# Readout of the memory as two rounded products, and a new order of the last stage's steps

## The reference, cut to what matters

```python
x = x + attention(_layernorm(x), ...)
x = x + xattn(_layernorm(x), ctx, mask)
x = x + ffn(_layernorm(x), ...)

def xattn(h, memory, mask):                      # h [8,512,512], memory [8,64,512]
    scores = einsum('bsd,bmd->bsm', h, memory) / sqrt(D)
    attn = softmax(where(mask, scores, -1e30))
    readout = einsum('bsm,bmd->bsd', attn, memory)
    return where(any(mask), readout, 0)

def ffn(x):
    qx, sx, sc = reorder_quantize(x)             # rounded to FP8, a scale for each row
    t = silu(qx @ w_gate) * (qx @ w_up)          # 1408 columns, each with its scale
    qt, st, sct = reorder_quantize(t)
    return qt @ w_down
```

## Time and profile before

| what | us |
|---|---|
| median of 3 runs | 2697.77 (2696.01 to 2700.08) |
| the profiled execution's own time | 2699.37 |
| its span | 2697.6 |
| mean granted TensorE clock | 0.991 of full |
| TensorE / VectorE / ScalarE / GpSimd busy | 2625.0 / 2123.9 / 1066.4 / 772.8 |

### The profile page before, as it was taken

One profiled execution on the slowest core, in us unless ns is written; L12 is line 12 of the kernel. 1 busy time (PEld: TensorE's weight loads), 2 busy tenths in 40 slices (PEclk: granted clock), 3 DMA queues, 4 the chain that ended last, 5 costly groups with the idle time before them and its releaser, 6 DMA issues.

```text
span 2697.6 us, 39827 instructions
## 1 busy us (share of the span) xinstructions
PE 2625.0 (97%) x14231; PEld 2173.0 (81%) x14231; DVE 2123.9 (79%) x3806; ACT 1066.4 (40%) x1786; POOL 772.8 (29%) x952
## 2 busy tenths in 40 slices
PE   6999899999999999999999999999999999999995
PEld 6888788888888888888888888888877666666662
DVE  7888977877787778778788867876657888888887
ACT  4433333433343343334344423433324445444553
POOL 3111211221131122112212211211123555555555
PEclk9999999999999999999999999999999999999998
DMA  6553322243233324343334422342265555555532
GB/s 230 180 212 141 128 104 104 102 163 121 102 136 131 122 100 137 105 147 119 126 111 147 157 94 94 118 180 94 94 227 173 148 157 161 151 147 160 162 99 54
DMA packets 182499, 366.67 MB, mean 136 GB/s; under 512 B 79264, under 2 KB 82208, under 8 KB 173600
## 3 DMA queue, kind: packets, MB, share of 16 engines
q1 hardware_dynamic: 116480, 339.74, 36.4%
q10 hardware_dynamic: 63488, 15.74, 3.2%
q0 software_dynamic: 2336, 8.65, 1.0%
HBM read 251.75 MB, written 96.61 MB: 129 GB/s over the span
## 4 chain that ended last, share of the span: by engine, by line
PE 95%; DVE 2%; issue 2%; POOL 0%; DMA 0%; ACT 0%; POOLq 0%; DVEq 0%; SPq 0%; ACTq 0%
PE bank L704 39%; PE bank L713 14%; PE bank L1356 13%; PE bank L828 9%; PE bank L788 9%; PE bank L1397 5%; PE bank L1407 2%; PE bank L1386 1%; PE bank L1377 1%; PE bank L1366 1%; PE bank L723 0%; PE bank L746 0%; DMA finish_xs<-in_pad_mask 0%; DVE finish_rt L1559 0%; DVE finish_u L1457 0%
## 5 line engine op out<-in xcount | busy, mean ns | idle before, releaser
L704 PE MATMUL bank<-attention_xT,attention_w_hi 128*128 128x512 f32 x3072 | 956.5, 392 | 2.7 <-DVE attention_xT L894 2.6
L704 PEld LDWEIGHTS bank<-attention_xT,attention_w_hi 128*128 128x128 f32 x3072 | 568.7, 189 | 114.5 <-issue 3.2
L704 PE MATMUL bank<-attention_xT,attention_w_lo 128*128 128x512 f32 x1536 | 599.6, 390 | 0.0
L531 POOL TENSOR_TENSOR attention_sq_sum<-attention_sq_sum,attention_sq 128x512 f32<-128x512 f32 x128 | 206.6, 1614 | 1228.9 <-ACT attention_sq L676 1228.9
L713 PE MATMUL bank<-attention_w_hi,attention_xT 128*128 128x256 f32 x2048 | 383.6, 288 | 3.7 <-DVE attention_sig_v L851 3.7
L704 PEld LDWEIGHTS bank<-attention_xT,attention_w_lo 128*128 128x128 f32 x1536 | 288.8, 188 | 62.1
L713 PEld LDWEIGHTS bank<-attention_w_hi,attention_xT 128*128 128x128 f32 x2048 | 321.1, 193 | 4.0 <-DVE attention_sig_v L851 4.0
L713 PE MATMUL bank<-attention_w_lo,attention_xT 128*128 128x256 f32 x1024 | 291.1, 284 | 0.0
L1356 PE MATMUL bank<-finish_w_out_hi,finish_og 128*128 128x512 f32 x824 | 284.7, 407 | 0.2
L984 DVE TENSOR_TENSOR attention_sf<-bank,attention_dcy 128x512 f32<-128x512 f32 (+1 forms) x256 | 147.8, 619 | 172.4 <-PE bank L788 172.3
L996 DVE TENSOR_TENSOR attention_sl<-attention_sf,attention_sh 128x384 fp32r<-128x384 f32 (+1 forms) x384 | 242.6, 686 | 0.0
(11 more groups left out here) (195 smaller groups left out, 4971.7 us busy)
## 6 DMA issues: line engine op xcount, KB each, us to landing
attention_xT<-normed_turned SPq DMA_DIRECT2D x62, 2048.0 KB, 8.5
gated_heads<-attention_og_out SPq DMA_DIRECT2D x64, 1024.0 KB, 7.3
finish_og<-gated_heads SPq DMA_DIRECT2D x103, 512.0 KB, 3.8
finish_og_last<-gated_heads SPq DMA_DIRECT2D x25, 512.0 KB, 3.8
normed_turned<-attention_shared SPq DMA_DIRECT2D x24, 512.0 KB, 6.6
attention_shared<-in_w_head SPq DMA_DIRECT2D x16, 512.0 KB, 7.1
finish_x<-in_x SPq DMA_DIRECT2D x32, 256.0 KB, 4.0
out<-finish_x SPq DMA_DIRECT2D x32, 256.0 KB, 4.3
```

The costliest lines, as they stand in the source:

```text
L531: g.tensor_tensor(sq_sum[:, col_b], sq_sum[:, col_b], sq[:, :], ALU.add).then_inc(s_acc, 1)
L704: mm = pe.matmul(dst[:, :], part[a][w][:, k, col:col + P], xT[i][:, b, k, :], start=(k == 0 and s == 0), stop=(k == KD - 1 and s == 2))
```

## The change

The readout [128 x 64] x [64 x 512] in F32 becomes two products in F32R that are 128 rows deep. The memory tile `mem` now has, in its lower 64 rows, the memory rounded to F32R, and in its upper 64 rows what that rounding leaves (low part). The numerators `pr` are written twice side by side ([128, 2, 64], by a second `exp`), so that their transpose has them in both halves; ScalarE copies it rounded to `pT[0]`, and VectorE subtracts that from the bank into `pT[1]` (`p_lo`). The readout is pT[0] by mem plus pT[1] by mem, in one bank. To fill `mem`, SP loads the memory's rows twice into `mem_raw`, ScalarE copies the upper half rounded into `mem[0:64]` and, 256 columns at a time, the other half into `mem_hi`, and VectorE subtracts (`mem_lo_of`); for batch 0 ahead of the loop, for later ones in two of the four steps before them.

The lists of TensorE, VectorE, ScalarE and GpSimd get a new order, and SP stores a tile one place earlier and loads x one place later. TensorE's step n is now: `scores(n+1)`, `gate_up(n-1,2)`, `down(n-3)`, `project(n+3,0)`, `turn_p(n+1)`, `project(n+3,1)`, `readout(n+1)`, `gate_up(n,0)`, `project(n+3,2)`, `gate_up(n,1)`, `turn_h(n+2)`, `project(n+3,3)`.

```diff
-    sc, pr, pT = sb("sc", [P, M]), sb("pr", [P, M]), sb("pT", [P, P])
+    pT = [sb(f"pT_{l}", [P, P], F32R) for l in ("hi", "lo")]
...
-    mem = [sb(f"mem{i}", [P, D]) for i in range(2)]
+    raw_at = Place(nc, "finish", sb.at, at.small)
+    mem_raw = [raw_at(f"mem_raw{i}", [P, D]) for i in range(2)]
+    mem = [sb(f"mem{i}", [P, D], F32R) for i in range(2)]
...
-            sp.dma_start(mem[b % 2][0:M, :], ctx_rows[b]).then_inc(s_mem[b % 2], 16)
+            for half in range(2):
+                sp.dma_start(mem_raw[b % 2][half * M:half * M + M, :], ctx_rows[b]).then_inc(s_mem[b % 2], 16)
...
-                if q == 2 and tile(n - 3):
+                if q == 1 and tile(n - 3):
                     store(n - 3)
-                if q == 1 and tile(n - 4) and n + 4 < T:
-                    sp.wait_ge(s_out, 16 * (n - 4) + 16)
-                    early.load_x(sp, n + 4)
+                if q == 3 and tile(n - 3) and n + 5 < T:
+                    sp.wait_ge(s_out, 16 * (n - 3) + 16)
+                    early.load_x(sp, n + 5)
...
+            nc.scalar.activation(pr[:, 0, :], sc[:, :], ACT.Exp, bias=sxm[:, 1:2],
+                                 accum_out=sxm[:, 2:3])
+            nc.scalar.activation(pr[:, 1, :], sc[:, :], ACT.Exp, bias=sxm[:, 1:2]).then_inc(s_exp, 1)
...
-            nc.scalar.copy(pT[0:M, :], X_BANK[0:M, 0:P]).then_inc(s_pTc, 1)
+            nc.scalar.copy(pT[0][:, :], X_BANK[:, 0:P]).then_inc(s_pTh, 1)
+
+        def mem_hi_of(b, part_):
+            a = part_ * (D // 2)
+            if part_ == 0:
+                act.wait_ge(s_mem[b % 2], 48 * (b // 2) + 48)
+                nc.scalar.copy(mem[b % 2][0:M, :], mem_raw[b % 2][0:M, :])
+            after(act, s_ml, 2 * b + part_)
+            nc.scalar.copy(mem_hi[M:2 * M, :], mem_raw[b % 2][M:2 * M, a:a + D // 2]).then_inc(s_mh, 1)
...
         attention_over(act)
+        mem_hi_of(0, 0)
+        mem_hi_of(0, 1)
...
-            pe.matmul(X_BANK[:, :], pT[0:M, :], mem[m // KT % 2][0:M, :], start=True, stop=True).then_inc(s_rd, 1)
+            pe.wait_ge(s_pTl, m + 1)
+            pe.wait_ge(s_ml, 2 * b + 2)
+            pe.matmul(X_BANK[:, :], pT[0][:, :], mem[b % 2][:, :], start=True, stop=False)
+            pe.matmul(X_BANK[:, :], pT[1][:, :], mem[b % 2][:, :], start=False, stop=True).then_inc(s_rd, 1)
...
+        def mem_lo_of(b, part_):
+            rows, a = slice(M, 2 * M), part_ * (D // 2)
+            v.wait_ge(s_mh, 2 * b + part_ + 1)
+            v.tensor_tensor(mem[b % 2][rows, a:a + D // 2], mem_raw[b % 2][rows, a:a + D // 2],
+                            mem_hi[rows, :].bitcast(F32), ALU.subtract).then_inc(s_ml, 1)
...
+        def p_lo(m):
+            v.wait_ge(s_pTh, m + 1)
+            after(v, s_rd, m)
+            v.tensor_tensor(pT[1][:, :], X_BANK[:, 0:P], pT[0][:, :].bitcast(F32), ALU.subtract).then_inc(s_pTl, 1)
...
         masks()
+        mem_lo_of(0, 0)
+        mem_lo_of(0, 1)
         early.root_of_squares(v)
```

More of the change, by code:

```diff
@@ L1248, in gpsimd @@
         g.wait_ge(s_k, 4)
-        for n in range(-3, T + 3):
+        for n in range(-2, T + 3):
+            if tile(n):
+                rstd3(n)
             if tile(n - 1):
+                silu_up(n - 1, 1)
                 silu_up(n - 1, 2)
+            if tile(n + 2):
+                rstd2(n + 2)
             if tile(n - 3):
                 add_ffn(n - 3)
-            if tile(n + 1):
-                rstd3(n + 1)
             if tile(n):
                 silu_up(n, 0)
[L1258 to L1261, removed]
     def scalar(act):
@@ L1319, in scalar @@
         attention_over(act)
+        mem_hi_of(0, 0)
+        mem_hi_of(0, 1)
         for n in range(-2, T + 2):
-            if tile(n):
-                x_turned(n)
             if tile(n + 1):
                 p_turned(n + 1)
+                next_mem(n + 1)
+            if tile(n - 2):
+                t_turned(n - 2)
             if tile(n - 1):
-                silu(n - 1, 1)
+                t_magnitude(n - 1)
             if tile(n + 2):
@@ L1329, in scalar @@
             if tile(n - 1):
-                silu(n - 1, 2)
-            if tile(n - 2):
-                t_turned(n - 2)
+                t_scaled(n - 1)
+            if tile(n):
+                silu(n, 0)
             if tile(n + 2):
@@ L1336, in scalar @@
                 x_scaled(n + 1)
-            if tile(n - 1):
-                t_magnitude(n - 1)
-                t_scaled(n - 1)
             if tile(n):
-                silu(n, 0)
+                silu(n, 1)
             if tile(n + 2):
                 exp(n + 2)
+            if tile(n + 1):
+                x_turned(n + 1)
+            if tile(n):
+                silu(n, 2)
     def tensor(pe):
@@ L1413, in tensor @@
             if tile(n - 1):
-                gate_up(n - 1, 1)
+                gate_up(n - 1, 2)
+            if tile(n - 3):
+                down(n - 3)
             if tile(n + 3):
                 project(n + 3, 0)
-            if tile(n - 1):
-                gate_up(n - 1, 2)
             if tile(n + 1):
@@ L1424, in tensor @@
                 readout(n + 1)
-            if tile(n - 3):
-                down(n - 3)
+            if tile(n):
+                gate_up(n, 0)
             if tile(n + 3):
@@ L1430, in tensor @@
                 early.sum_squares(pe)
+            if tile(n):
+                gate_up(n, 1)
             if tile(n + 2):
@@ L1434, in tensor @@
                 project(n + 3, 3)
-            if tile(n):
-                gate_up(n, 0)
     def vector(v):
@@ L1531, in softmax, with next_mem @@
             v.tensor_scalar(sxm[:, 1:2], sxm[:, 0:1], -1.0, None, ALU.mult).then_inc(s_max, 1)
+        def mem_lo_of(b, part_):
[3 more added lines that the diff above has]
+                            mem_hi[rows, :].bitcast(F32), ALU.subtract).then_inc(s_ml, 1)
+        def next_mem(m):
+            if m % KT >= 2 and m // KT + 1 < B:
+                mem_lo_of(m // KT + 1, m % KT - 2)
+        def p_lo(m):
+            v.wait_ge(s_pTh, m + 1)
+            after(v, s_rd, m)
+            v.tensor_tensor(pT[1][:, :], X_BANK[:, 0:P], pT[0][:, :].bitcast(F32), ALU.subtract).then_inc(s_pTl, 1)
         def denominator(m):
@@ L1581, in vector @@
         masks()
+        mem_lo_of(0, 0)
+        mem_lo_of(0, 1)
         early.root_of_squares(v)
-        for n in range(-3, T + 2):
-            if tile(n + 1):
-                x_scale(n + 1)
+        for n in range(-2, T + 3):
+            if tile(n - 2):
+                t_round_sum(n - 2)
+            if tile(n + 2):
+                add_attention(n + 2)
+            if tile(n):
+                x_round_sum(n)
+            if tile(n + 1):
+                softmax(n + 1)
+            if tile(n):
+                x_round_out(n)
+            if tile(n - 1):
+                scaled_gate_up(n - 1, 2)
+            if tile(n - 2):
+                t_round_out(n - 2)
+            if tile(n - 3):
+                y_scaled(n - 3)
+            if tile(n + 2):
+                norm2_stats(n + 2)
+            if tile(n + 1):
+                p_lo(n + 1)
+                denominator(n + 1)
             if tile(n - 1):
                 t_scale(n - 1)
-            if tile(n + 3):
-                add_attention(n + 3)
             if tile(n + 1):
-                x_round_sum(n + 1)
+                add_readout(n + 1)
+                next_mem(n + 1)
+            if tile(n):
+                gate_up_scale(n)
+            if tile(n + 1):
+                norm3_stats(n + 1)
             if n == 0:
@@ L1595, in vector @@
                 scaled_gate_up(n, 0)
-            if tile(n + 2):
-                softmax(n + 2)
             if tile(n + 1):
-                x_round_out(n + 1)
+                centred(n + 1)
+                x_scale(n + 1)
             if tile(n):
                 scaled_gate_up(n, 1)
[L1602 to L1620, removed]
     programs = Shared()
```

18 lines of the change are left out of this document (10 added, 8 removed).

## The result

The changed kernel takes 2680.31 us (median of 4 runs, 2678.15 to 2681.50) against 2698.65 for the kernel before (4 runs): a ratio of 0.9935 (95% interval 0.9922 to 0.9948), 18.3 us less. Intervals stand in square brackets from here on. The prediction was 2679.5 us, 2671 to 2691, faster with 0.88.

A forecast was written before the change was run, and what follows sets the result against it. TensorE's instructions were taken to bound the last stage until project(31) ends, VectorE and latencies the drain. Savings of 21.1 us, 3.7 lost at the start and 1.0 net gained in the drain gave 2679.4 us, range 2671 to 2691.

The forecast's parts named there:

- The readout: TensorE's readout in each step: two F32R products at 0.229 us make 0.46 for 1.05, saving 0.59 a step.
- the products are not single-pass: Rival, 2%: the two readout products cost 1.05 us each, so the kernel gets slower, 2728 us.
- What follows the readout: TensorE behind the readout: down loses 0.10 us by following gate_up; four early projections lose 0.21 each.
- Do the other engines keep that step: Steady step: VectorE, GpSimd and ScalarE fit TensorE's 20.00 us; tightest is p_lo, 1.9 us early for the readout.
- the walk: Steady step's new lists laid out with old durations: TensorE ends at 20.0 us, VectorE's t_round_sum at 19.8.
- partial waits: Rival, 17%: TensorE stays first but stops some 0.3 us a step, at the readout's waits or late ScalarE; 2688 us.
- VectorE becomes the bound: Rival, 6%: collisions with GpSimd make VectorE's p_lo late for the readout; slower, step 21.55 us, 2725 us.
- Start of the stage: a cost: At the last stage's start, VectorE's memory subtractions ahead of rs_out make TensorE start 3.7 us later.
- once again and no more: After TensorE's gap at the stage's start, the lowered clock loses about 1.7 us, as before the change.
- The drain: After project(31): 4.5 us shorter; with 3.5 us moved ahead of it, net -1.0, ends -2.5 and +2.
- Sum: Whole kernel: -21.1 + 3.7 - 1.0 = -18.4 us, so 2679.4 us beside the median.
- Where a rule speaks against the change: VectorE's roundings against GpSimd: x_round_out gets free of a 0.71 us wait, x_round_sum may get it, sum unchanged.

The follow-up runs named there:

- products_twice: The changed kernel with the readout's pair of products issued twice into the same sums; 2694.52 us, 14.2 more than the change.
- products_only: The kernel before with the two F32R readout products but all engine lists in the old order; 2682.48 us, ratio 0.9940.
- order_only: The new order of all lists with the old F32 readout of 64 rows; 2696.64 us, ratio 0.9995 to the kernel before.
- vector_plus1: The changed kernel with one extra 1408-column reduction on VectorE ahead of p_lo in each step; 2685.51 us.
- vector_plus3: The changed kernel with three extra 1408-column reductions on VectorE ahead of p_lo in each step; 2778.2 us, one run.
- after_again: The changed kernel itself, measured again on one chip with two variants; 2680.37 us, ratio 0.9930 to the kernel before.
- mem_after_root: The changed kernel with batch 0's mem_lo_of moved behind rs_out, add_attention(0) and norm2_stats(0); 2675.53 us, again 2673.91.
- root_first: The changed kernel with batch 0's mem_lo_of and the masks both moved behind norm2_stats(0); 2677.29 us.
- loads_later: The changed kernel with masks and batch 0's mem_lo_of behind norm2_stats(0), and SP's first feed-forward weight and second memory loads later; 2672.50 us, again 2670.46.

## Why the prediction was right

**The readout.** Right: 0.46 us from the projection's own matmul, against the bounds 0.46 and 1.05. products_twice confirms it as a price. So the rival "the products are not single-pass" falls. The change took the readout from F32 to F32R and from 64 rows to 128 at once; how much of the saving is owed to each, no run tells.

**What follows the readout.** Right in size (2.37, all 0.1 of it gone). The reason was only half put: the prediction said that down is free because it now follows gate_up. products_only shows down at 2.39 right behind the F32R products, order_only shows the 0.09 at gate_up behind an F32 one. So what counts is the product ahead and not the place. Which of its properties is open: type and depth changed together, and F32 alone does not do it, since scores are F32 too and the gate_up behind them takes 1.73 and 1.30 (after), no longer than elsewhere.

**Do the other engines keep that step.** Right: p_lo ends at 2334.25 and the readout starts at 2336.36, 2.1 us early for a predicted 1.9, the walk's tightest. VectorE took less than the walk gave it, since x_round_out got free of GpSimd and x_round_sum all but (0.81 us for the walk's 1.3). It even stands 0.95 us for pT_hi ahead of p_lo, so what sets p_lo's time in the step is turn_p and ScalarE's copy, and not VectorE's list:

```profile
2326.94 0.81 DVE L1532 SCALAR_TENSOR_TENSOR finish_xs<-finish_xa,finish_xs 128x512 f32<-128x512 bf16 x1
...
2328.26 0.69 DVE L1538 SCALAR_TENSOR_TENSOR finish_q<-finish_xa,finish_xs 128x512 bf16<-128x512 bf16 x1
...
2333.96 0.29 DVE L1571 TENSOR_TENSOR finish_pT_lo<-bank,finish_pT_hi 128x128 fp32r<-128x128 f32 x1 [0.95 <-ACT finish_pT_hi L1311]
```

The rivals "partial waits" and "VectorE becomes the bound" fall by the step of 20.00. vector_plus1 bears 1.6 us more with a collision of 0.6, vector_plus3 no longer bears 4.9 with one of 0.9; by its step the point from which the second rival decides is, as an estimate, 4.9 + 0.9 - 2.9 = 2.9 us. The prediction had 2.0, from 18.0 us of VectorE's work that it doesn't derive; its own terms, 17.22 + 0.28 + 0.20, leave 2.3.

**Start of the stage: a cost.** Right in sign and place, but 2.7 us for 3.7 (3.2 in after_again). The memory half landed 5.6 us after its issue, not 7.2, and so 1.5 us earlier behind the first mark; the copies and subtractions behind it took 2.6 us for 2.1:

```profile
1994.57 5.63 DMA finish_mem_raw<-in_ctx
...
2000.31 0.62 ACT finish_mem L1318
...
2001.44 0.43 DVE finish_mem L1561
```

The same step's "once again and no more" on the half clock did not hold in this trace: in before 4.1 us at 0.58, here 5.2 us at 0.50. The first 36 matmuls take 10.87 us for 10.05 in before, +0.8. It is no fixed price of the longer gap: in after_again TensorE had stood for 6.95 us, and these matmuls take as long as in before; the last section has the rows. Another 0.4 us, in both traces of the change, are lost to a cause that the prediction did not have, the first transposed q16:

```profile
2036.51 4.84 DMA finish_qT<-finish_q
...
2041.39 1.90 PE bank L1422 x8
```

It took twice the 2.4 us of the earlier trace rows; the slack of 4.7 us for it was read from the steady step. In the first one TensorE has no gate_up(n-1,2) and no down yet (1.30 and 2.37 us of that slack), and SP's loads run beside it. In before this first transfer took 4.9 us as well, with nothing waiting for it. Where it didn't hold TensorE up, in mem_after_root, the stretch from restart to project(31) is 1.3 us shorter, this 0.4 and the 0.8 together.

**The drain.** -5.6 us for -4.5, so -2.1 net of the 3.5 that moved ahead (predicted -1.0, inside its ends). What makes the further 1.1 was not tested apart, and most of it does not repeat: after_again, the same kernel, has 70.87, so -4.8. order_only, which has no products, has -4.65: nearly all of the shorter drain comes from the order.

**Sum.** To project(31): -21.1 + 3.5 + 0.8 + 0.4 = -16.4, measured -16.5; in after_again -21.1 + 3.5 + 0.4 = -17.2, measured -17.3. With +2.7 and -5.6 the traces have -19.4 and the medians -18.3 for a predicted -18.4: the errors of the start (1.0 too much, 1.2 not foreseen) cancelled, and the drain's 1.1 stands against the difference of traces and medians. The mechanism and the 21.1 were right; that the whole difference was met to 0.1 us is luck, since single stretches of the same kernel differ by up to 0.8 us from trace to trace.

**Where a rule speaks against the change.** The runs bear out its sign: x_round_out took 1.40 us, and takes 0.69 in the new order (712 ns mean of 32). Little took its place: x_round_sum, which the walk had let have it, went from a mean of 682 ns to 823. The Trainium skill ("SBUF — State Buffer", Who interferes with whom) says that a VectorE instruction with two SBUF inputs and a GpSimd one that reads SBUF exclude each other. vector_plus3 agrees, with x_round_sum at 1.70.

## What to carry to other kernels

Where one engine is busy all the time, price a cheaper instruction on it by its neighbours' duration in the chain and multiply: that came out to 0.1 us in 21, in both traces of the change. The rest of the error sits where the steady step is not: at a stage's start, cost a new wait by the transfer behind it, and look at what else the queues carry then, since an earlier engine only meets the next late transfer. Look for the new part's first use: it need not stand ahead of work that the bounding engine waits for (mem_after_root, 3.0 to 3.4 us by the traces).

## What the runs showed that was not expected

- The old readout, F32 and 64 rows deep, costs the instruction behind it too, whatever that is: +0.21 us on a projection, +0.10 on down, +0.09 on gate_up (order_only). Behind the F32R products there is no such loss (2.39 for down in products_only), and behind the F32 scores gate_up has none either.
- Single-column instructions of GpSimd are held up whole by a rounding of VectorE. rstd2's nine took 5.4 us before and 2.7 here (2333.15 to 2335.86). Before, the first took 1.50 us instead of 0.19 and ended with t_round_sum (2401.51 to 2403.12), the fifth took 1.62 and ended with t_round_out:

```profile
2333.15 0.19 POOL L1219 TENSOR_TENSOR finish_newton<-finish_mv,finish_kf 128x1 f32<-128x1 f32 x1
...
2335.67 0.19 POOL L1236 TENSOR_TENSOR finish_neg_mean_rstd<-finish_neg_mean_rstd,finish_kf 128x1 f32<-128x1 f32 x1
```

  This is most of GpSimd's 3.2 us: its busy time had held time in which it stood still.
- The transposing transfer of q16 took 2.4 us in the median, 4.8 beside a load of down's weights and 7.4 in root_first; in loads_later, where the load of down comes later, the first takes 2.5. The same instruction, other traffic.
- The half clock by the length of the stop, from the granted clock in stretches of 1 us. After 1.2 us (loads_later) it did not fall. After 3.8 us (before) it fell at the restart and was half for 3.4 us, all of it worked in. After 6.4 (the change) and 6.95 us (after_again) it fell during the stop and was half for 6.8 us, of which 5.2 and 3.5 were worked in. Six traces with stops of 6.2 to 7.0 us lose 0 to 0.8 us more than before in the first 36 matmuls.
